# A two-layer transformer block on one core: each chunk's gelu made twice from its PSUM bank instead of once and cast

## The chip, the cores and the metric

The kernel runs on one core of one Trainium2 chip. The metric is the device time of one execution in microseconds (us), lower is better.

## The reference, cut to what matters

8192 tokens (128 sequences of 64) of width 256 pass through two layers. Each has a modulated layer norm, attention with 16 heads over the 64 tokens of a sequence, a projection with a residual, a second modulated norm and a feed-forward part of width 1024 (the second layer rotates queries and keys too):

```python
z = z * (1.0 + gamma2[:, None, :]) + beta2[:, None, :]
z = jax.nn.gelu(z @ fc1_w + fc1_b, approximate=False) @ fc2_w + fc2_b
x = x + z * alpha2[:, None, :]
```

## The kernel before

A tile is 512 tokens, so there are 16 tiles in each layer, numbered 0 to 31 through both. Each engine has one hand-written program; semaphores join them, and the order of the work on an engine is the order of the calls in its `step`. Step u does three things side by side: attention of tile u, the feed-forward part of tile u-1 (its last back product falls in step u+1), and the norm and the query, key and value products of tile u+1. Steps are unrolled at the ends of a layer and looped between. The argument named `a` is the layer of tile u+1, `b` that of tile u, `c` that of tile u-1, and None where there is no such tile.

Every matrix product is done in three passes: operands are split into a high part, rounded to fp32r, and a low part, the rest; high by high, high by low and low by high are added.

The hidden layer goes in 8 chunks of 128 channels. For chunk m:

- PE's `hidden` (L1086; its matmuls stand under L912) makes 6 matmuls of 512 columns into bank C, the only bank for it. It waits until the gelu of chunk m-1 has read C (semaphore `gelu`).
- ACT's `hidden` (L754) makes `hact` from C with the bias, at L757. `hact`, `h_hi` and `h_lo` hold two chunks each, in turn.
- ACT's `hidden_high` (L759) casts `hact` to `h_hi` at L762. It waits on the gelu's semaphore and on the back product of chunk m-2.
- POOL's `hidden_low` (L556) makes `h_lo = hact - h_hi` at L559.
- PE's `back` (L1095) makes 12 matmuls of 256 columns into banks D: 8 with `h_hi`, then, after a wait for `h_lo`, 4 with it (L1106).

In ACT's `step`, the cast stands right behind its gelu for chunks 1, 5, 6 and 7. For chunks 0, 2, 3 and 4 there is other work between. What matters around them:

- `high_heads` (L777) writes the high part of the turned heads, `ot_hi`, from bank E; DVE's `low_heads` (L1406) then writes `ot_lo`, and PE's `project` (L912, into E) waits for both.
- `exponential` (L766) of one half-group of attention scores, before PE's `turn_probs` (L1050) transposes them into B.
- `move_probs` (L771) copies the turned probabilities out of B to `probs_turned`; PE's `weigh_values` (L1064) waits for it.
- `high_qk` (L738 in the first layer) writes `q_flat` or `k_flat`; DVE's `low_qk` (L1345) follows, and holds what stands behind it on DVE.

PE runs, around chunks 0 and 1: `hidden` 0, `project` 0, two `first_turn`s, `turn_heads` 1, `hidden` 1, `project` 1, `back` 0, `hidden` 2. Around chunk 3: `hidden` 3, `turn_probs` (2,0), `queries_keys` 1, `turn_probs` (2,1), `back` 2, `weigh_values` (2,0) and (2,1).

Of the kernel before, what the change touches and what calls it, by code (L numbers as in the profile page):

```python
# [34 lines left out]
ACT = mybir.ActivationFunctionType  # L35
# [7 lines left out]
MC = FF // P  # L43
# [23 lines left out]
def build(nc, t, out):  # L67

    ctx = ExitStack()
    with ctx:  # L70
        def sb(name, shape, dt=F32):
            return ctx.enter_context(nc.sbuf_tensor(name, shape, dt))

        def bank(name):
            return ctx.enter_context(nc.psum_tensor(name, [P, 512], F32))

        def sem(name):
            return ctx.enter_context(nc.semaphore(name))
# [46 lines left out]
        hact = sb("hact", [P, 2, TILE])  # L125
        hb = [sb("h_hi", [P, 2, TILE], F32R), sb("h_lo", [P, 2, TILE], F32R)]
# [8 lines left out]
        b1_col = sb("b1_col", [P, 2, MC])  # L135
# [35 lines left out]
        C = bank("C")  # L171
# [37 lines left out]
        pe_f1, gelu, h_hi, h_lo, pe_f2 = sem("pe_f1"), sem("gelu"), sem("h_hi"), sem("h_lo"), sem("pe_f2")  # L209
# [5 lines left out]
        def upto(u, n, k):  # L215
            return u * n + k

        def known(u):
            return isinstance(u, int)

        def await_(eng, semaphore, count):

            if not (known(count) and count <= 0):
                eng.wait_ge(semaphore, count)
# [288 lines left out]
        def _(pool):  # L513
# [42 lines left out]
            def hidden_low(tile, m):  # L556
                await_(pool, pe_f2, upto(tile, MC, m - 1))
                pool.wait_ge(h_hi, upto(tile, MC, m + 1))
                pool.tensor_tensor(hb[1][:, m % 2, :], hact[:, m % 2, :], hb[0][:, m % 2, :].bitcast(F32),  # L559
                                   ALU.subtract).then_inc(h_lo, 1)  # L560

# [46 lines left out]
            def step(u, n, a, b, c, p):  # L608
                if c is not None:
                    second_rstd(u - 1, G - 1)  # L610
                if p is not None:
                    hidden_low(u - 2, MC - 2)
# [46 lines left out]
        def _(act):  # L659
# [43 lines left out]
            def second_norm(tile, g):  # L703
                await_(act, pe_zt, upto(tile - 1, 2, g // 2 + 1))
                act.wait_ge(ln2_rstd, upto(tile, G, g + 1))
                nc.scalar.activation(zn[:, g, :], x_res[:, g, :], ACT.Identity, scale=rs2[:, g:g + 1],
                                     bias=nb2[:, g:g + 1]).then_inc(zn_ready, 1)
# [44 lines left out]
                        nc.scalar.copy(dst, src).then_inc(v_moved, 1)  # L752

            def hidden(tile, layer, m):  # L754
                act.wait_ge(pe_f1, upto(tile, MC, m + 1))
                await_(act, h_lo, upto(tile, MC, m - 1))
                nc.scalar.activation(hact[:, m % 2, :], C[:, :], ACT.Gelu, bias=b1_col[:, layer, m:m + 1]).then_inc(gelu, 1)  # L757

            def hidden_high(tile, m):  # L759
                act.wait_ge(gelu, upto(tile, MC, m + 1))  # L760
                await_(act, pe_f2, upto(tile, MC, m - 1))
                nc.scalar.copy(hb[0][:, m % 2, :], hact[:, m % 2, :]).then_inc(h_hi, 1)  # L762

            def exponential(u, g, b):
                act.wait_ge(s_sub, upto(u, 2 * G, 2 * g + b + 1))
                nc.scalar.activation(exps[:, b, :], exps[:, b, :], ACT.Exp, scale=SCORE_SCALE).then_inc(s_exp, 1)  # L766
# [13 lines left out]
            def step(u, n, a, b, c, p):  # L780
                if p is not None:
                    hidden(u - 2, p, MC - 1)
                    hidden_high(u - 2, MC - 1)
                if c is not None:
                    second_norm(u - 1, G - 1)
                if b is not None:
                    exponential(u, 0, 0)
                if c is not None:
                    second_high(u - 1, 0)
                if b is not None:  # L790
                    exponential(u, 0, 1)
                    move_probs(u, 0, 0)
                    move_probs(u, 0, 1)
                if known(u) and u == NT:
                    act.wait_ge(pe_proj, upto(NT, G, 0))
                    high_weights(1, 1)
                if known(u) and u == NT + 1:
                    high_piece(2, 1, 3)
                    high_piece(3, 1, 2)
                if b is not None:  # L800
                    exponential(u, 1, 0)
                    exponential(u, 1, 1)
                    move_probs(u, 1, 0)
                if c is not None:
                    second_high(u - 1, 1)
                if b is not None:
                    move_probs(u, 1, 1)
                    high_heads(u, b, 0)
                if known(u) and u == NT + 1:
                    high_piece(3, 1, 3)  # L810
                if c is not None:
                    hidden(u - 1, c, 0)
                if b is not None:
                    high_heads(u, b, 1)
                if c is not None:
                    hidden_high(u - 1, 0)
                if c is not None:
                    hidden(u - 1, c, 1)
                    hidden_high(u - 1, 1)
                if a is not None:  # L820
                    first_high(u + 1, 0)
                if b is not None:
                    second_norm(u, 0)
                if a is not None:
                    first_high(u + 1, 1)
                if c is not None:
                    hidden(u - 1, c, 2)
                if b is not None:
                    exponential(u, 2, 0)
                    second_norm(u, 1)  # L830
                    exponential(u, 2, 1)
                if c is not None:
                    hidden_high(u - 1, 2)
                if a == 0:
                    high_qk(u + 1, 0, 0)
                if c is not None:
                    hidden(u - 1, c, 3)
                if b is not None:
                    move_probs(u, 2, 0)
                if a == 0:  # L840
                    high_qk(u + 1, 0, 1)
                if b is not None:
                    move_probs(u, 2, 1)
                if c is not None:
                    hidden_high(u - 1, 3)
                if a == 1:
                    high_qk(u + 1, 1, 0)
                if b is not None:
                    exponential(u, 3, 0)
                if a == 0:  # L850
                    high_qk(u + 1, 0, 2)
                if b is not None:
                    high_heads(u, b, 2)
                if a == 1:
                    high_qk(u + 1, 1, 1)
                if b is not None:
                    move_probs(u, 3, 0)
                    exponential(u, 3, 1)
                if a == 0:
                    high_qk(u + 1, 0, 3)  # L860
                if known(u) and u == NT:
                    high_piece(2, 1, 0)
                    high_piece(2, 1, 1)
                if c is not None:
                    hidden(u - 1, c, 4)
                if b is not None:
                    move_probs(u, 3, 1)
                if a == 1:
                    high_qk(u + 1, 1, 2)
                if c is not None:  # L870
                    hidden_high(u - 1, 4)
                if b is not None:
                    second_norm(u, 2)
                if a == 1:
                    high_qk(u + 1, 1, 3)
                if a is not None:
                    values(u + 1, 0)
                if c is not None:
                    hidden(u - 1, c, 5)
                    hidden_high(u - 1, 5)  # L880
                if b is not None:
                    high_heads(u, b, 3)
                if known(u) and u == NT:
                    high_piece(3, 1, 0)
                if a is not None:
                    values(u + 1, 1)
                if c is not None:
                    hidden(u - 1, c, 6)
                    hidden_high(u - 1, 6)
                if known(u) and u == NT - 2:  # L890
                    act.wait_ge(pe_v, upto(NT, 2, 0))
                    high_weights(0, 1)
                if known(u) and u == NT:
                    high_piece(3, 1, 1)
                    high_piece(2, 1, 2)
                if n is not None:
                    first_norm(u + 2)
                    first_columns(u + 2, n)
                if b is not None:
                    second_columns(u, b)  # L900
# [729 lines left out]
```

## Time and profile before

| | |
|---|---|
| median of 3 runs | 1885.76 us (1884.67 to 1885.84) |
| the profiled execution's own time | 1885.72 us |
| its span | 1883.9 us |
| granted clock | 0.986 |
| PE busy / DVE / ACT / POOL | 95% / 66% / 69% / 45% |

The span runs from the first to the last instruction of the profiled execution; 1.8 us of its time lie outside. Times in rows are from the span's start. PE is the matmul engine, PEld its weight loads, ACT the scalar engine, DVE the vector engine. A busy share is an average over steps, and says little by itself where an engine waits.

### The profile page before, as it was taken

What the parts mean: (1) busy time and instruction counts of PE and PEld (TensorE: products, weight loads), DVE (VectorE), ACT (ScalarE), POOL (GpSimd) and SP (SyncE); (2) the same over time, 40 slices, a digit from 0 to 9 for tenths busy, and PEclk for the clock granted to TensorE, in tenths of its full rate; (3) what the DMA queues carried; (4) which work ended last, traced back from release to release, by engine and by line L of the source; (5) the groups of instructions that cost most, each with busy time, mean ns of one, the idle gap of its engine ahead of it and who ended that gap; (6) DMA issues with size and microseconds to landing.
All of it is one profiled execution on the core that took longest, in us unless ns stands there. A gap on an engine that the chain in (4) does not pass through costs nothing.

```text
span 1883.9 us, 41740 instructions
## 1 busy us (share of the span) xinstructions
PE 1788.1 (95%) x12623; PEld 1637.1 (87%) x12623; DVE 1237.4 (66%) x2985; ACT 1306.7 (69%) x2327; POOL 849.4 (45%) x1036
## 2 busy tenths in 40 slices
PE   4779999999999999999899999999999999999998
PEld 3668888888988888988889999999999999999986
DVE  4756667667667667666867667667667766666751
ACT  4337777777776776776668776776776677777663
POOL 2123333333333343333456655555665555566534
PEclk8889999999999999999999999999999999999999
DMA  6463435454434444344454233334323333333320
GB/s 166 107 147 95 100 97 133 117 128 111 97 96 119 122 122 122 89 105 108 124 149 109 84 108 98 98 107 114 84 86 105 101 103 106 103 84 97 93 71 34
DMA packets 330276, 199.84 MB, mean 106 GB/s; under 512 B 160995, under 2 KB 314597, under 8 KB 330213
## 3 DMA queue, kind: packets, MB, share of 16 engines
q1 hardware_dynamic: 330212, 199.06, 40.0%
q8 instruction: 32, 0.52, 0.1%
q14 instruction: 32, 0.25, 0.0%
HBM read 80.98 MB, written 17.33 MB: 52 GB/s over the span
## 4 chain that ended last, share of the span: by engine, by line
PE 73%; DVE 12%; issue 8%; SPq 2%; ACT 2%; DMA 1%; POOL 1%; DVEq 0%; POOLq 0%; ACTq 0%
PE D L1106 17%; PE C L912 16%; PE B L912 9%; PE B L1064 9%; PE A L1031 7%; PE B L1050 5%; PE A L912 5%; PE E L912 4%; DVE mx L1373 2%; SPq L329 2%; DVE o_sb L1397 2%; PE A L1036 2%; DVE exps L1379 1%; DVE ot_lo L1406 1%; PE E L1075 1%
## 5 line engine op out<-in xcount | busy, mean ns | idle before, releaser
L559 POOL TENSOR_TENSOR h_lo<-hact,h_hi 128x512 fp32r<-128x512 f32 x256 | 330.4, 1291 | 302.6 <-ACT h_hi L762 289.5
L1031 PE MATMUL A<-k_pad,q_pad 128*128 128x256 f32 x1536 | 259.9, 296 | 14.3 <-DVE exps L1379 9.3
L1106 PE MATMUL D<-wgt_hi,h_hi 128*128 128x256 f32 x1024 | 263.4, 290 | 0.0
L771 ACT COPY probs_turned<-B 128x512 f32<-128x512 f32 x256 | 147.7, 584 | 157.7 <-PE B L1050 157.7
L1064 PE MATMUL B<-v_blocks,probs_turned 128*128 128x68 f32 x2048 | 255.8, 272 | 0.4 <-ACT probs_turned L771 0.4
L1106 PE MATMUL D<-wgt_lo,h_hi 128*128 128x256 f32 x1024 | 255.7, 282 | 0.0
L1064 PEld LDWEIGHTS B<-v_blocks,probs_turned 128*128 128x128 f32 x2048 | 250.3, 193 | 5.8 <-ACT probs_turned L771 2.5
L757 ACT ACTIVATE hact<-C,b_col 128x512 f32<-128x512 f32 x256 | 176.1, 688 | 96.0 <-PE C L912 92.1
L1031 PEld LDWEIGHTS A<-k_pad,q_pad 128*128 128x128 f32 x1536 | 214.8, 194 | 18.3 <-issue 9.5
L1373 DVE TENSOR_REDUCE mx<-A 128x8 f32<-128x512 f32 x256 | 174.3, 681 | 69.3 <-PE A L1036 39.4
L766 ACT ACTIVATE exps<-exps 128x512 f32<-128x512 f32 x256 | 160.9, 630 | 76.3 <-DVE exps L1379 75.7
L1106 PEld LDWEIGHTS D<-wgt_lo,h_hi 128*128 128x128 f32 x1024 | 195.4, 191 | 1.4
L1106 PEld LDWEIGHTS D<-wgt_hi,h_hi 128*128 128x128 f32 x1024 | 194.7, 190 | 2.1 <-ACT h_hi L762 0.4
L1379 DVE TENSOR_TENSOR exps<-A,mx 128x512 f32<-128x512 f32 x256 | 174.1, 680 | 4.0 <-PE B L1050 0.7
L912 PE MATMUL C<-z_hi,wgt_hi 128*128 128x512 f32 x512 | 168.9, 411 | 5.3 <-ACT hact L757 4.8
L549 POOL TENSOR_SCALAR rs<-mv 128x1 f32<-128x1 f32 x128 | 28.3, 221 | 316.0 <-DVE mv L1430 304.7
L1106 PE MATMUL D<-wgt_hi,h_lo 128*128 128x256 f32 x1024 | 166.6, 285 | 1.5 <-POOL h_lo L559 1.3
L1050 PE MATMUL B<-ident,exps 128*128 128x128 f32 x1024 | 157.5, 277 | 6.4 <-DVE q_flat L1345 1.4
L762 ACT CAST h_hi<-hact 128x512 fp32r<-128x512 f32 x256 | 159.4, 623 | 4.2
L1397 DVE TENSOR_TENSOR o_sb<-B,rden 64x128 f32<-64x128 f32 x512 | 146.5, 286 | 23.1 <-PE E L1075 5.8
L912 PE MATMUL C<-z_hi,wgt_lo 128*128 128x512 f32 x512 | 159.8, 393 | 0.0
L912 PE MATMUL C<-z_lo,wgt_hi 128*128 128x512 f32 x512 | 158.8, 391 | 0.0
(140 smaller groups left out, 3944.0 us busy)
## 6 DMA issues: line engine op xcount, KB each, us to landing
k_pad<-k_flat SPq DMA_DIRECT2D x512, 64.0 KB, 2.1
q_pad<-q_flat SPq DMA_DIRECT2D x256, 128.0 KB, 2.3
gates<-gates SPq DMA_DIRECT2D x64, 256.0 KB, 4.5
x_bias<-x_bias SPq DMA_DIRECT2D x32, 512.0 KB, 3.5
rotation<-rotation SPq DMA_DIRECT2D x256, 64.0 KB, 1.9
x_in<-in_x SPq DMA_DIRECT2D x16, 512.0 KB, 4.2
gates<-gated_bias SPq DMA_DIRECT2D x32, 256.0 KB, 5.0
x_res<-in_x SPq DMA_DIRECT2D x16, 512.0 KB, 4.4
```

Of the source, the lines that this page charges most:

```text
L559: pool.tensor_tensor(hb[1][:, m % 2, :], hact[:, m % 2, :], hb[0][:, m % 2, :].bitcast(F32), ALU.subtract).then_inc(h_lo, 1)
L757: nc.scalar.activation(hact[:, m % 2, :], C[:, :], ACT.Gelu, bias=b1_col[:, layer, m:m + 1]).then_inc(gelu, 1)
L762: nc.scalar.copy(hb[0][:, m % 2, :], hact[:, m % 2, :]).then_inc(h_hi, 1)
L766: nc.scalar.activation(exps[:, b, :], exps[:, b, :], ACT.Exp, scale=SCORE_SCALE).then_inc(s_exp, 1)
L912: ins = nc.tensor.matmul(dst, l[p], r[q], start=(p, q) == order[0] and n == 0, stop=(p, q) == order[-1] and n == len(pairs) - 1)
L1031: ins = nc.tensor.matmul(dst, qpad[g % 2][:, c, p, b, :, :].rearrange("p x s -> p (x s)"), kpad[g % 2][:, c, q, :, b * S:(b + 1) * S], sta ...
L1050: ins = nc.tensor.transpose(B[b][:, n * P:(n + 1) * P], exps[:, b, n * P:(n + 1) * P], ident[:, :])
L1064: ins = nc.tensor.matmul(B[b][:, n * 68:(n + 1) * 68], pt[:, b, n * P:(n + 1) * P], moving, start=True, stop=True)
L1106: ins = nc.tensor.matmul(Dk[g // 2][:, (g % 2) * D:(g % 2 + 1) * D], hb[p][:, m % 2, g * P:(g + 1) * P], w_slice(q, W_FF2, D, m, 0, D), st ...
L1373: nc.vector.tensor_reduce(mx[:, b, :], A[b][:, :].rearrange("p (h k) -> p h k", k=S), AX.X, ALU.max)\
L1379: nc.vector.tensor_tensor(exps[:, b, :].rearrange("p (h k) -> p h k", k=S), A[b][:, :].rearrange("p (h k) -> p h k", k=S), mx[:, b, :].rea ...
L1397: ins = nc.vector.tensor_tensor(o_sb[p, b, :].rearrange("p (n j d) -> p n j d", n=4, j=2), sums_of(b)[p, :, x, :, 0:HD], rden[p, b, :].rea ...
```

## The change

ACT's `hidden` now reads bank C twice. The first gelu writes `h_hi` directly, rounded, and signals `h_hi`; the second writes `hact`, unrounded, and signals `gelu`, which frees C. `hidden_high` with its cast is gone, and so are its eight call sites. The first gelu takes the wait for the back product of chunk m-2 that the cast had; the second keeps the wait for `h_lo` of chunk m-2. POOL's `hidden_low` waits for both gelus.

```diff
             def hidden_low(tile, m):
                 await_(pool, pe_f2, upto(tile, MC, m - 1))
                 pool.wait_ge(h_hi, upto(tile, MC, m + 1))
+                pool.wait_ge(gelu, upto(tile, MC, m + 1))
...
             def hidden(tile, layer, m):
+
                 act.wait_ge(pe_f1, upto(tile, MC, m + 1))
+                await_(act, pe_f2, upto(tile, MC, m - 1))
+                nc.scalar.activation(hb[0][:, m % 2, :], C[:, :], ACT.Gelu, bias=b1_col[:, layer, m:m + 1]).then_inc(h_hi, 1)
                 await_(act, h_lo, upto(tile, MC, m - 1))
                 nc.scalar.activation(hact[:, m % 2, :], C[:, :], ACT.Gelu, bias=b1_col[:, layer, m:m + 1]).then_inc(gelu, 1)
-
-            def hidden_high(tile, m):
-                act.wait_ge(gelu, upto(tile, MC, m + 1))
-                await_(act, pe_f2, upto(tile, MC, m - 1))
-                nc.scalar.copy(hb[0][:, m % 2, :], hact[:, m % 2, :]).then_inc(h_hi, 1)
...
                 if b is not None:
                     high_heads(u, b, 1)
                 if c is not None:
-                    hidden_high(u - 1, 0)
-                if c is not None:
                     hidden(u - 1, c, 1)
-                    hidden_high(u - 1, 1)
...
                 if b is not None:
                     move_probs(u, 2, 1)
-                if c is not None:
-                    hidden_high(u - 1, 3)
```

The other call sites go the same way. The first place is on ACT in the loop of the first layer, around chunk 0: the gelu out of C, the heads' high part (`ot_hi`) and the cast, and then chunk 1's gelu. Before:

```order
L757 ACT_TABLE_LOAD
L757 ACTIVATE hact<-C,b_col 128x512 [waits h_lo]
L774 REGISTER_ALU
L777 ACTIVATE ot_hi<-E,v_bias 128x128 [waits pe_proj,pe_ot]
L777 ACTIVATE ot_hi<-E,v_bias 128x128
L762 CAST h_hi<-hact 128x512 [waits pe_f2,gelu]
L755 REGISTER_ALU
L757 ACTIVATE hact<-C,b_col 128x512 [waits h_lo,pe_f1]
```

And now:

```order
L759 ACT_TABLE_LOAD
L759 ACTIVATE h_hi<-C,b_col 128x512 [waits pe_f2]
L761 ACTIVATE hact<-C,b_col 128x512 [waits h_lo]
L773 REGISTER_ALU
L776 ACTIVATE ot_hi<-E,v_bias 128x128 [waits pe_proj,pe_ot]
L776 ACTIVATE ot_hi<-E,v_bias 128x128
L757 REGISTER_ALU
L759 ACTIVATE h_hi<-C,b_col 128x512 [waits pe_f2,pe_f1]
```

The second reading of C has moved in front of the heads, and the cast behind them is gone.

The second place is ACT in the same loop around chunk 3: the gelu, the two copies of turned probabilities with a key chunk (`k_flat`) between them, the cast, and the next exponential. Before:

```order
L757 ACT_TABLE_LOAD [waits h_lo]
L757 ACTIVATE hact<-C,b_col 128x512 [waits pe_f1]
L771 COPY probs_turned<-B 128x512 [waits pe_pv,pe_pt]
L736 REGISTER_ALU
L738 ACTIVATE k_flat<-A,qk_bias 128x4x128 [waits pe_qk]
L771 COPY probs_turned<-B 128x512 [waits pe_pv,pe_pt]
L762 CAST h_hi<-hact 128x512 [waits pe_f2,gelu]
L765 REGISTER_ALU
L766 ACT_TABLE_LOAD
L766 ACTIVATE exps<-exps 128x512 [waits s_sub]
```

And now:

```order
L759 ACT_TABLE_LOAD [waits pe_f2]
L759 ACTIVATE h_hi<-C,b_col 128x512 [waits pe_f1]
L761 ACTIVATE hact<-C,b_col 128x512 [waits h_lo]
L770 COPY probs_turned<-B 128x512 [waits pe_pv,pe_pt]
L737 REGISTER_ALU
L739 ACTIVATE k_flat<-A,qk_bias 128x4x128 [waits pe_qk]
L770 COPY probs_turned<-B 128x512 [waits pe_pv,pe_pt]
L764 REGISTER_ALU
L765 ACT_TABLE_LOAD
L765 ACTIVATE exps<-exps 128x512 [waits s_sub]
```

A gelu has come in ahead of both copies and the key chunk, and the cast behind them is gone. The number of table loads in the program is the same, 54.

## Rows read from the trace of the kernel before

**Rows 1.** The page: busy time, and the chain that ended last

```profile
PE 1788.1 (95%) x12623; PEld 1637.1 (87%) x12623; DVE 1237.4 (66%) x2985; ACT 1306.7 (69%) x2327; POOL 849.4 (45%) x1036
PE 73%; DVE 12%; issue 8%; SPq 2%; ACT 2%; DMA 1%; POOL 1%; DVEq 0%; POOLq 0%; ACTq 0%
```

**Rows 2.** Groups by line on ACT (busy us, mean ns, idle before)

```profile
L757 ACT ACTIVATE hact<-C,b_col 128x512 f32<-128x512 f32 x256 | 176.1, 688 | 96.0 <-PE C L912 92.1 <-POOL h_lo L559 1.5
L762 ACT CAST h_hi<-hact 128x512 fp32r<-128x512 f32 x256 | 159.4, 623 | 4.2
```

**Rows 3.** Waits of PE after 960 us (total, times, longest)

```profile
PE C L912 <- ACT hact L757: 4.8, 15, 0.8
...
PE D L1106 <- POOL h_lo L559: 0.7, 3, 0.2
```

**Rows 4.** Timeline of ACT, second layer, chunk 0 (start, us long)

```profile
1314.84 0.69 ACT L757 ACTIVATE hact<-C,b_col 128x512 f32<-128x512 f32 x1
1315.43 0.62 ACT L777 ACTIVATE ot_hi<-E,v_bias 128x128 fp32r<-128x128 f32 x2
```

**Rows 5.** Timeline of PE, second layer, `hidden` 1 in two steps

```profile
1093.73 0.74 PE L912 MATMUL C<-z_hi,wgt_hi 128*128 128x512 f32 x2 [0.24 <-ACT hact L757]
...
1315.59 0.73 PE L912 MATMUL C<-z_hi,wgt_hi 128*128 128x512 f32 x2 [0.24 <-ACT hact L757]
```

**Rows 6.** Timeline, first layer, chunk 0: ACT, then PE's `hidden` 1

```profile
411.66 0.69 ACT L757 ACTIVATE hact<-C,b_col 128x512 f32<-128x512 f32 x1
...
413.46 0.71 PE L912 MATMUL C<-z_hi,wgt_hi 128*128 128x512 f32 x2
```

**Rows 7.** Timeline of ACT, first layer, from chunk 2's cast on

```profile
422.82 0.60 ACT L762 CAST h_hi<-hact 128x512 fp32r<-128x512 f32 x1
...
425.32 0.69 ACT L757 ACTIVATE hact<-C,b_col 128x512 f32<-128x512 f32 x1
425.91 0.58 ACT L771 COPY probs_turned<-B 128x512 f32<-128x512 f32 x1
...
426.95 0.59 ACT L771 COPY probs_turned<-B 128x512 f32<-128x512 f32 x1
```

**Rows 8.** Timeline of PE in the same stretch

```profile
426.95 1.90 PE L1064 MATMUL B<-v_blocks,probs_turned 128*128 128x68 f32 x16
...
427.80 1.05 PE L1064 MATMUL B<-v_blocks,probs_turned 128*128 128x68 f32 x8
...
433.45 0.65 PE L1050 MATMUL B<-ident,exps 128*128 128x128 f32 x4
```

**Rows 9.** Timeline of DVE in the same stretch

```profile
427.11 0.75 DVE L1345 SCALAR_TENSOR_TENSOR k_flat<-A,qk_bias,k_flat 128x512 fp32r<-128x512 f32 x1 [2.31 <-ACT k_flat L738]
428.00 0.21 DVE L1389 RECIPROCAL rden<-B 128x8 f32<-128x8 f32 x1
...
432.57 0.75 DVE L1345 SCALAR_TENSOR_TENSOR q_flat<-B,qk_bias,q_flat 128x512 fp32r<-128x512 f32 x1 [1.28 <-ACT q_flat L738]
```

**Rows 10.** Timeline, first layer, step's start, PE

```profile
454.86 0.63 PE L1050 MATMUL B<-ident,exps 128*128 128x128 f32 x4
...
467.08 0.48 PE L912 MATMUL E<-wgt_hi,ot_hi 128*128 128x256 f32 x2 [0.89 <-DVE ot_lo L1406]
```

**Rows 11.** Timeline of the last 65 us: PE, then ACT

```profile
1823.41 0.63 PE L1050 MATMUL B<-ident,exps 128*128 128x128 f32 x4 [0.38 <-ACT exps L766]
...
1855.18 0.73 PE L912 MATMUL C<-z_hi,wgt_hi 128*128 128x512 f32 x2 [0.78 <-ACT hact L757]
...
1858.10 0.63 PE L912 MATMUL C<-z_hi,wgt_hi 128*128 128x512 f32 x2
...
1854.44 0.69 ACT L757 ACTIVATE hact<-C,b_col 128x512 f32<-128x512 f32 x1 [1.75 <-PE C L912]
1855.16 0.62 ACT L762 CAST h_hi<-hact 128x512 fp32r<-128x512 f32 x1
1856.88 0.69 ACT L757 ACTIVATE hact<-C,b_col 128x512 f32<-128x512 f32 x1 [1.09 <-PE C L912]
```

More of the change, by code:

```diff
@@ L782, in step @@
                     hidden(u - 2, p, MC - 1)
-                    hidden_high(u - 2, MC - 1)
                 if c is not None:
@@ L831, in step @@
                     exponential(u, 2, 1)
-                if c is not None:
-                    hidden_high(u - 1, 2)
                 if a == 0:
@@ L843, in step @@
                     move_probs(u, 2, 1)
-                if c is not None:
-                    hidden_high(u - 1, 3)
                 if a == 1:
@@ L869, in step @@
                     high_qk(u + 1, 1, 2)
-                if c is not None:
-                    hidden_high(u - 1, 4)
                 if b is not None:
@@ L879, in step @@
                     hidden(u - 1, c, 5)
-                    hidden_high(u - 1, 5)
                 if b is not None:
@@ L888, in step @@
                     hidden(u - 1, c, 6)
-                    hidden_high(u - 1, 6)
                 if known(u) and u == NT - 2:
```

## Prediction, made before the changed kernel ran

> **What bounds the kernel now.** I read the busy shares and the chain first. PE is busy for 95% of the span, and the chain that ended last lies on PE for 73% and on DVE for 12%; ACT has 2% of it [rows 1]. So the time is PE's, and an edit on ACT counts only where PE waits for it, or where it comes to. Next the waits of PE. In the first layer none is for a gelu. After 960 us there are 15 waits for the gelu that frees bank C, 4.8 us in all [rows 3]. The timeline shows where. In the second layer PE's `hidden` 1 starts at 1315.59, 0.24 us idle, and the gelu of chunk 0 ends at 1314.84 + 0.69 = 1315.53 [rows 4, 5]. The same row with the same idle stands in each of twelve steps, from 1093.73 on [rows 5]; the other three are in the last 65 us, one of them at 1855.18 [rows 11]. So in those steps the wait on bank C already ends last, with nothing in reserve. In the first layer the gelu of chunk 0 ends at 411.66 + 0.69 = 412.35 and PE uses C again at 413.46, 1.11 us later [rows 6].
>
> **What the change removes and adds on ACT.** It takes away 256 casts of 623 ns and adds 256 gelus out of the bank of 688 ns [rows 2]. The trace has no gelu behind a gelu. An instruction behind one starts 0.59 us after it if it waits for nothing (425.32 to 425.91 [rows 7], 1314.84 to 1315.43 [rows 4]); where it waits for the gelu's semaphore, as the cast does, it starts 0.72 us after (1854.44 to 1855.16 [rows 11]). The second gelu waits for no result of the first, so I take 0.59, and 0.72 is the upper bound. A cast cost ACT its 0.60 [rows 7] less the 0.10 by which an unhindered successor begins before the end (425.32 + 0.69 - 425.91), so 0.50. Per chunk that is +0.09 where other work stood between, and 0.13 less, -0.04, where the cast stood right behind. ACT's load is thus the same; what changes is where the time lies.
>
> The Trainium skill's page "ScalarE: Activation LUTs" (section "What ACT_TABLE_LOAD costs") gives an ACTIVATE with a pointer bias 280 ns + 0.833 ns per column, and an overlap of 93 ns between two in a row. That is 706 - 93 = 613 ns for the added gelu, an estimate from the page; the row says 590 and stands. By the page the sum below would be 0.6 us larger.
>
> Who gets what: the high part comes sooner everywhere, and the low part about as soon as before in chunks 1, 5, 6, 7 and sooner in the others. PE hardly waits for either, so this earns next to nothing. The price is that bank C, and everything behind the gelu on ACT, is released 0.59 us later. The wait for the back product of chunk m-2, now ahead of the first gelu, costs nothing: PE issues that product before `hidden` m, whose end the gelu waits for anyway.
>
> **Second layer, chunk 0.** PE's `hidden` 1 starts when the second gelu ends: 1314.84 + 0.59 + 0.69 = 1316.12, and 0.06 for the start, 1316.18 instead of 1315.59: +0.59. Behind the gelu on ACT stand the heads' high parts, due at 1315.43; 0.59 later they are still ready for `project` 1, which PE reaches after `hidden` 1, itself 0.59 later. PE runs almost without a gap after that, and what DVE, POOL and the DMAs do for it next starts from PE's own products, so they shift with it. Twelve steps: 12 x 0.59 = **7.1 us** (upper bound 12 x 0.72 = 8.6).
>
> **First layer, chunk 0.** 1.11 us of cover against 0.59: nothing.
>
> **First layer, chunk 3.** Here the gelu holds up the copies of turned probabilities. ACT arrives at the gelu of chunk 3 later by 0.59 (second gelu of chunk 2) less 0.50 (its cast, gone from 422.82 [rows 7]) = 0.09. Then a second gelu: the copies and the key chunk between them all come 0.59 + 0.09 = 0.68 later. The first copy ends at 425.91 + 0.58 = 426.49 and PE's `weigh_values` starts at 426.95; the second ends at 426.95 + 0.59 = 427.54 and its matmuls start at 427.80 [rows 7, 8]. Cover of 0.46 and 0.26 is less than 0.68: PE's second block starts at 427.54 + 0.68 + 0.05 = 428.27, +0.47. DVE says the same: its `low_qk` waits for the key chunk (2.31 us idle), goes from 427.11 to 427.79 and ends at 428.54, and the reciprocal behind it, at 428.00 [rows 9], starts at about 428.5, +0.5. I take 0.47. From there the chain runs over the normalised heads, the next maximum and subtraction, the exponential and the query chunk to DVE's `low_qk` at 432.57 [rows 9], for which PE waits before it turns probabilities at 433.45 [rows 8]. So the 0.47 reaches PE again and isn't taken back. After this PE runs gapless to the start of the next step, and DVE's long chain there starts from PE's first scores. Steps 1 to 14 have this order (the loop and its two unrolled ends): 14 x 0.47 = **6.6 us**. Lower bound 0, if that cover is larger than I read; upper 14 x 0.68 = 9.5.
>
> In the second layer ACT has no key chunk between the copies, since `high_qk` stands later, and they come early enough: nothing.
>
> **First layer, step's start.** ACT has no idle time before the first exponential, and two gelu-cast pairs stand in that stretch, so it comes about 0.1 us sooner, and PE waits for it at 454.86. But PE waits 0.89 us for DVE at 467.08 [rows 10]; DVE works without a gap from the first scores on. What PE gains at 454.86 it waits longer at 467.08: nothing.
>
> **The end, after 1822 us.** PE waits for the exponential at 1823.41 [rows 11], which comes 0.59 later, and for the copy behind it, 0.68 later in all: +0.7. Three waits for the gelu, of 15 [rows 3], grow by 0.59 each: +1.8. In the last tile nothing but the feed-forward part is left. There the gelu of chunk 1 ends at 1856.88 + 0.69 = 1857.57 and PE needs C at 1858.10 [rows 11]: cover of 0.53 against 0.59 + 0.05. So chunks 1, 2, 5 and 6 wait about 0.1 each: +0.4. The last two low parts come 0.05 sooner: -0.1. Together **+2.8 us**, bounds 2 and 4.5.
>
> **Sum.** 7.1 + 6.6 + 2.8 = 16.5 us. The profiled execution took 1885.72 us (span 1883.9, 1.8 outside), which is the median 1885.76 within its own scatter. 1885.7 + 16.5 = 1902.2; I say **1902 us**, 0.9% slower.
>
> The page "PSUM — Partial Sum Buffer" of the Trainium skill (summary of rules) says to evacuate promptly. It speaks against this change, and the trace agrees: bank C is the one that PE waits for at 1315.59.
>
> **Rivals.**
> *A: the first layer's stall is covered.* For it: the cover of 0.46 and 0.26 is no small part of 0.68, and DVE was 2.31 us idle before that chunk. Against it: DVE's own queue arrives at the same +0.47. Time: 1885.7 + 7.1 + 2.8 = 1895.6. Chance 0.10.
> *B: the second gelu doesn't overlap the first.* 0.72 instead of 0.59 in 12 + 14 steps and some 6 places of the end: 32 x 0.13 = 4.2 more, 1906. For it: only different instructions are seen behind a gelu. Chance 0.10.
> *C: not slower, by the sooner `h_hi` and `h_lo`.* PE has some waits for `h_lo`, 0.7 us in all in the second layer [rows 3], and the first layer's first exponential comes sooner. It decides only if bank C isn't held longer, so if both readings together end no later than the one gelu, which 2 x 0.69 less an overlap of 0.10 rules out unless the second reading is shortened. Time: 0.7 + 14 x 0.1 = 2.1 less, 1884, or a little below. Chance 0.03.
> *D: no difference.* PE is later at chunk 0, but catches up in the same step at waits that are set by something which doesn't shift. Against it: the rows show PE without such waits in the second layer. Time 1886. Chance 0.03.
> My forecast has the rest, 0.74, and its own range is 1898 to 1905.
>
> **How the numbers follow.** 0.2% of 1886 us, 3.8 us, is about what a measurement of this kernel can tell from no change. Range: from A, 1895.6 with its end at the lower bound, 1895, to B, 1906, plus a little for the end: 1895 to 1907. It leaves out C and D and the tails, under 2 in 10. Slower 0.94; same 0.04 (D, and a part of C); faster 0.02 (the rest of C).
>
> **What the new profile would show.** Right: the second gelu starts 0.59 after the first; in twelve steps of the second layer PE idles about 0.8 us before `hidden` 1, for `hact`; in steps 1 to 14 PE waits for `probs_turned` at `weigh_values` (2,1); steps of the first layer are 0.47 us longer, and those of the second 0.59 (four of them now take 1315.59 - 1093.73 = 221.9 us [rows 5], which becomes 224.2). Wrong, if the step length of either layer is unchanged, or if POOL or DVE became what PE waits for.

## The result, and the profile after

The changed kernel takes 1900.09 us (median of 4 runs, 1898.91 to 1900.92). The kernel before, run on the same chip, takes 1885.22 us (median of 4, 1884.59 to 1885.84). The ratio is 1.0077, with a 95% interval of 1.0063 to 1.0090: 14.9 us slower. Forecast were 1902 us and slower. The profiled execution of the changed kernel has a span of 1897.5 us, 13.6 us more than before; the granted clock of TensorE has the same mean of 0.986 in both, so the clock explains nothing of it.

The changed kernel's page first: busy times, then the chain that ended last, then the two groups of `hidden` on ACT (busy us, mean ns of one, idle time before and what ended it).

```profile
PE 1792.6 (94%) x12623; PEld 1639.3 (86%) x12623; DVE 1235.9 (65%) x2985; ACT 1307.9 (69%) x2327; POOL 850.1 (45%) x1036
...
PE 67%; DVE 12%; issue 10%; ACT 7%; SPq 3%; DMA 1%; POOL 1%; DVEq 0%; ACTq 0%; POOLq 0%
...
L759 ACT ACTIVATE h_hi<-C,b_col 128x512 fp32r<-128x512 f32 x256 | 176.3, 689 | 137.4 <-PE C L899 134.0
L761 ACT ACTIVATE hact<-C,b_col 128x512 f32<-128x512 f32 x256 | 174.4, 681 | 0.0
```

ACT has the same number of instructions as before and is busy for 1.2 us more in 1307.9: its load is not what costs. Its share of the chain that ended last went from 2% to 7% [rows 1]. The second group has no idle time before it, so the second reading of the bank always stands right behind the first. The next rows are the first lines of PE's waits after 960 us in the changed kernel (total us, times, longest).

```profile
PE C L899 <- ACT hact L761: 13.3, 15, 1.4
...
PE B L1051 <- ACT probs_turned L770: 1.0, 1, 1.0
```

The same 15 waits for the gelu as before, 8.5 us more in all [rows 3]. The timeline at the first of the two places, second layer, chunk 0: ACT, then PE.

```profile
1320.00 1.28 ACT L759 ACT_TABLE_LOAD   x1 [1.71 <-PE C L899]
1321.30 0.69 ACT L759 ACTIVATE h_hi<-C,b_col 128x512 fp32r<-128x512 f32 x1
1321.88 0.68 ACT L761 ACTIVATE hact<-C,b_col 128x512 f32<-128x512 f32 x1
1322.45 0.63 ACT L776 ACTIVATE ot_hi<-E,v_bias 128x128 fp32r<-128x128 f32 x2
```

```profile
1322.61 0.73 PE L899 MATMUL C<-z_hi,wgt_hi 128*128 128x512 f32 x2 [0.81 <-ACT hact L761]
1323.18 0.63 PE L899 MATMUL C<-z_hi,wgt_lo 128*128 128x512 f32 x2
1323.65 0.62 PE L899 MATMUL C<-z_lo,wgt_hi 128*128 128x512 f32 x2
1324.11 0.40 PE L899 MATMUL E<-wgt_hi,ot_hi 128*128 128x256 f32 x2
1324.35 0.40 PE L899 MATMUL E<-wgt_lo,ot_hi 128*128 128x256 f32 x2
```

The second gelu starts 0.58 us after the first and ends at 1322.56; PE's `hidden` 1 starts 0.05 later, 0.81 us idle instead of 0.24 [rows 5].

The second place, first layer, chunk 3, on ACT, PE and DVE:

```profile
426.64 0.69 ACT L759 ACTIVATE h_hi<-C,b_col 128x512 fp32r<-128x512 f32 x1
427.23 0.68 ACT L761 ACTIVATE hact<-C,b_col 128x512 f32<-128x512 f32 x1
427.80 0.58 ACT L770 COPY probs_turned<-B 128x512 f32<-128x512 f32 x1
428.26 0.71 ACT L739 ACTIVATE k_flat<-A,qk_bias 128x512 fp32r<-128x512 f32 x1
428.85 0.60 ACT L770 COPY probs_turned<-B 128x512 f32<-128x512 f32 x1
```

```profile
426.68 0.36 PE L1093 MATMUL D<-wgt_hi,h_hi 128*128 128x256 f32 x1
...
428.53 2.08 PE L1051 MATMUL B<-v_blocks,probs_turned 128*128 128x68 f32 x16 [0.17 <-ACT probs_turned L770]
...
435.16 0.65 PE L1037 MATMUL B<-ident,exps 128*128 128x128 f32 x4
```

```profile
429.01 0.75 DVE L1332 SCALAR_TENSOR_TENSOR k_flat<-A,qk_bias,k_flat 128x512 fp32r<-128x512 f32 x1 [2.90 <-ACT k_flat L739]
429.68 0.20 DVE L1376 RECIPROCAL rden<-B 128x8 f32<-128x8 f32 x1
```

`weigh_values` (2,0) now waits 0.17 us for the first copy, and the 16 matmuls of (2,0) and (2,1) take 2.08 instead of 1.90 us [rows 8]. The ninth matmul, the first of (2,1), starts at 429.50, 0.05 after the end of the second copy. About 0.11 of the 0.18 lies there and 0.07 at the first matmul: a short wait in the middle of a group shows as a longer group. DVE was idle for 2.90 us before the key chunk instead of 2.31 [rows 9].

How long is a step? The start of the gelu of chunk 0 in `hact` marks it. Two such rows, ten steps apart, first for the first layer and then for the second (ACT):

```profile
244.38 0.68 ACT L761 ACTIVATE hact<-C,b_col 128x512 f32<-128x512 f32 x1
...
808.05 0.68 ACT L761 ACTIVATE hact<-C,b_col 128x512 f32<-128x512 f32 x1
...
1154.01 0.68 ACT L761 ACTIVATE hact<-C,b_col 128x512 f32<-128x512 f32 x1
...
1713.83 0.68 ACT L761 ACTIVATE hact<-C,b_col 128x512 f32<-128x512 f32 x1
```

(808.05 - 244.38) / 10 = 56.37 us, and (1713.83 - 1154.01) / 10 = 55.98. The same rows of the kernel before stand at 243.85, 803.18, 1148.48 and 1703.15, which makes 55.93 and 55.47. So a step of the first layer is 0.44 us longer and one of the second 0.51. Added up over the trace, with each tile's first gelu as the mark (in the changed kernel the one into `h_hi`, 0.58 us ahead of the other; the steps have the same length by either): the steps into tiles 1 to 13 +5.7, those into tiles 14 to 17 (the change of layer) -0.3, the twelve of the second layer +6.1, from the first gelu of tile 29 to the end of the program +3.0, and the time before tile 0's first gelu -0.9. That is the span's 13.6. The -0.9 at the start isn't the change's, since no changed instruction runs before that gelu; over the kernels below, chunk 0's gelu of tile 1 stands anywhere between 185.3 and 189.3 us. The change of layer scatters too: e12 below runs the same instructions there as the changed kernel, and its steps into tiles 14 to 17 are 1.2 us longer than before where the changed kernel's are 0.3 shorter. Without the start the terms make 14.5, beside 14.9 by the medians.

In the last 65 us these waits of PE have grown:

```profile
1837.59 0.63 PE L1051 MATMUL B<-v_blocks,probs_turned 128*128 128x68 f32 x4 [1.00 <-ACT probs_turned L770]
...
1848.76 0.73 PE L899 MATMUL C<-z_hi,wgt_hi 128*128 128x512 f32 x2 [0.92 <-ACT hact L761]
...
1867.52 0.73 PE L899 MATMUL C<-z_hi,wgt_hi 128*128 128x512 f32 x2 [1.36 <-ACT hact L761]
...
1881.49 0.73 PE L899 MATMUL C<-z_hi,wgt_hi 128*128 128x512 f32 x2 [1.36 <-ACT hact L761]
```

The wait of 0.78 at 1855.18 [rows 11] is the one that now stands at 1867.52 with 1.36 us: +0.58, one second gelu. The kernel before has the other two at 1836.99 (0.34) and 1868.21 (0.78), and each grew by 0.58 as well.

### The profile page after: what moved, and what is told of

Same layout as the page of the kernel before. It is cut to its first block, busy times and chain, and to the rows that moved or that the text cites. A ratio compares the mean times of both kernels' runs of the same rounds, so it can differ in the third digit from the quotient of the medians.

```text
span 1897.5 us, 41684 instructions
## 1 busy us (share of the span) xinstructions
PE 1792.6 (94%) x12623; PEld 1639.3 (86%) x12623; DVE 1235.9 (65%) x2985; ACT 1307.9 (69%) x2327; POOL 850.1 (45%) x1036
## 4 chain that ended last, share of the span: by engine, by line
PE 67%; DVE 12%; issue 10%; ACT 7%; SPq 3%; DMA 1%; POOL 1%; DVEq 0%; ACTq 0%; POOLq 0%
PE C L899 15%; PE D L1093 14%; PE B L899 9%; PE B L1051 9%; PE A L1018 7%; PE E L899 4%; PE B L1037 4%; PE A L899 3%; SPq L329 2%; DVE mx L1360 2%; ACT hact L761 2%; DVE o_sb L1384 2%; PE A L1023 1%; DVE exps L1366 1%; DVE ot_lo L1393 1%
## 5 line engine op out<-in xcount | busy, mean ns | idle before, releaser
L759 ACT ACTIVATE h_hi<-C,b_col 128x512 fp32r<-128x512 f32 x256 | 176.3, 689 | 137.4 <-PE C L899 134.0
```

What stands on the lines that cost most here:

```text
L759: nc.scalar.activation(hb[0][:, m % 2, :], C[:, :], ACT.Gelu, bias=b1_col[:, layer, m:m + 1]).then_inc(h_hi, 1)
```

## The experiments

All were timed in five rounds beside the kernel before, and compared by ratio. Step lengths are read as above, ten steps apart, from each kernel's own trace. The theory is that of the prediction: three places, and at each of them a delay by one gelu. Here are all twelve together; "longer" is the ratio less 1, times 1885.5 us, the middle of the medians of the kernel before.

| kernel | median us | ratio, 95% interval | longer, us | step, first layer | step, second layer |
|---|---|---|---|---|---|
| before | 1885.2 to 1886.0 | | | 55.93 | 55.47 |
| changed | 1900.09 | 1.0077 [1.0063, 1.0090] | +14.5 | 56.37 | 55.98 |
| e1 chunk 0 by cast | 1893.63 | 1.0045 [1.0031, 1.0058] | +8.5 | 56.36 | 55.47 |
| e2 chunk 3 by cast | 1893.35 | 1.0042 [1.0028, 1.0056] | +7.9 | 55.91 | 56.00 |
| e3 chunks 0, 3 by cast | 1885.83 | 1.0003 [0.9994, 1.0012] | +0.6 | 55.91 | 55.47 |
| e4 second gelu 3 late | 1893.46 | 1.0040 [1.0026, 1.0053] | +7.5 | 55.91 | 55.99 |
| e5 bank held only | 1892.81 | 1.0037 [1.0025, 1.0050] | +7.0 | 55.91 | 55.97 |
| e6 delay only | 1889.76 | 1.0026 [1.0016, 1.0036] | +4.9 | 56.34 | 55.46 |
| e7 changed, table early | 1894.00 | 1.0050 [1.0037, 1.0063] | +9.4 | 56.33 | 55.48 |
| e8 e4, table early | 1887.09 | 1.0008 [0.9999, 1.0017] | +1.5 | 55.87 | 55.44 |
| e9 before, table early | 1885.35 | 1.0000 [0.9991, 1.0009] | 0 | 55.89 | 55.49 |
| e10 e9, low heads first | 1877.74 | 0.9961 [0.9947, 0.9975] | -7.4 | 55.58 | 55.19 |
| e11 e8, low heads first | 1877.92 | 0.9960 [0.9946, 0.9974] | -7.5 | 55.59 | 55.20 |
| e12 end by cast | 1898.15 | 1.0062 [1.0048, 1.0076] | +11.7 | 56.37 | 55.99 |

**e1, e2 and e3: undo one part of the change.** In the chunks of `CAST` the high part is the cast of before again, at its old place; the others read the bank twice. e1 has `CAST = (0,)`, e2 `(3,)`, e3 `(0, 3)`.

```diff
+                if m not in CAST:
+                    await_(act, pe_f2, upto(tile, MC, m - 1))
+                    nc.scalar.activation(hb[0][:, m % 2, :], C[:, :], ACT.Gelu, ...).then_inc(h_hi, 1)
...
+            def hidden_high(tile, m):
+                if m in CAST:
+                    act.wait_ge(gelu, upto(tile, MC, m + 1))
+                    await_(act, pe_f2, upto(tile, MC, m - 1))
+                    nc.scalar.copy(hb[0][:, m % 2, :], hact[:, m % 2, :]).then_inc(h_hi, 1)
```

> The changed kernel, with chunk 0 alone made in the old way (one gelu out of bank C, and the cast at its old place); the other seven chunks read the bank twice. My theory: the second layer's loss is the bank held 0.58 us longer at chunk 0, in 12 steps, so PE's wait before hidden 1 falls from 0.81 to 0.24 us there, and one of the waits in the last tile too: 1900.1 - 12 x 0.51 - 0.6 = 1893.4 us. The first layer's steps stay 56.37 us long. Rival, that any chunk's second reading costs its share alike (14.9 us over eight chunks): 1900.1 - 1.9 = 1898.2.

> The changed kernel, with chunk 3 alone made in the old way. My theory: the first layer's loss is the 0.68 us by which the copies of turned probabilities and the key chunk behind the gelu of chunk 3 come later, so its steps fall from 56.37 to 55.93 us in 14 steps, and the second layer's stay at 56.0: 1900.1 - 14 x 0.44 = 1893.9, some 0.5 less with what it gives at the end, 1893.5 us. Rival, an equal share for each chunk: 1898.2. Rival A of the prediction (that stall is covered, and the 6 us came from elsewhere in the first layer): 1900.

> The changed kernel, with chunks 0 and 3 made in the old way. My theory: both losses of the steady steps go, 12 x 0.51 + 14 x 0.44 + 1.1 at the end = 13.4 of the 14.9 us: 1886.7 us, with steps of 55.93 and 55.47 us as before, and what is left lies after 1822 us. Rival, an equal share for each chunk: 1900.1 - 3.7 = 1896.4.

Measured: 1893.63, 1893.35 and 1885.83 us. The step lengths separate cleanly. With chunk 0 by cast the second layer's step is that of before (55.47) and the first layer's stays long; with chunk 3 by cast it is the other way round; with both, six of eight chunks read the bank twice and the time is 0.6 us longer by the ratio, with an interval of -1.1 to +2.3 that holds no difference. So in the steady steps the double reading costs nothing where it has cover, and the two losses are separate and add up. What is left lies at the end: from tile 29's first gelu on, e3 takes 1.9 us longer than before.

**e4: all chunks twice, but chunk 3's second gelu late.** It stands where the cast stood, behind the two copies and the key chunk.

```diff
+                if m not in LATE:
+                    gelu_low(tile, layer, m)
...
+            def hidden_high(tile, layer, m):
+                if m in LATE:
+                    gelu_low(tile, layer, m)
```

> Every chunk reads the bank twice, but chunk 3's second gelu stands where its cast stood, behind both copies and the key chunk. Bank C isn't wanted again for 10.9 us there. If the loss of the first layer is the place in ACT's queue, its steps fall to 55.93 us: 1900.1 - 14 x 0.44 - 0.5 = 1893.5 us, as with the cast. Rival, that it is the second reading of the bank itself, or ACT's 65 ns more per chunk: no change, 1900.

Measured: 1893.46 us. The first layer's step is back at 55.91, although bank C is read twice in every chunk and, at chunk 3, held longer than in the changed kernel. ACT in that stretch:

```profile
424.84 0.69 ACT L765 ACTIVATE h_hi<-C,b_col 128x512 fp32r<-128x512 f32 x1
425.42 0.58 ACT L784 COPY probs_turned<-B 128x512 f32<-128x512 f32 x1
425.89 0.70 ACT L739 ACTIVATE k_flat<-A,qk_bias 128x512 fp32r<-128x512 f32 x1
426.47 0.59 ACT L784 COPY probs_turned<-B 128x512 f32<-128x512 f32 x1
426.94 0.72 ACT L759 ACTIVATE hact<-C,b_col 128x512 f32<-128x512 f32 x1
```

The first copy starts 0.58 us after the gelu again (0.59 before), instead of 1.16. At chunk 3 it is the queue on ACT that costs, not the bank.

**e5: hold the bank, and nothing else.** The kernel before; in the second layer PE's `hidden` 1 also waits for the heads' high part, which ACT makes right behind the gelu.

```diff
-            def hidden(tile, m):
+            def hidden(tile, m, held=False):
...
+                if m == 1 and held:
+                    pe.wait_ge(ot_hi, upto(tile + 1, 8, 4))
...
-                    hidden(u - 1, 1)
+                    hidden(u - 1, 1, held=c == 1 and b is not None)
```

> The kernel before with one wait more: in the second layer PE's hidden 1 (the first write of bank C after chunk 0's gelu) also waits for ot_hi of heads 1, which ACT ends about 0.51 us after that gelu. ACT's instructions and their order are those of before, so only the bank is held longer. Theory of the prediction (in the second layer the loss is the bank held at chunk 0): 12 steps of about 0.5 us, 1885.6 + 6.1 = about 1891.5 us. Rival (the loss is ACT's queue moved later, ot_hi and what follows it, and not the bank): 1885.6 us, no difference.

Measured: 1892.81 us; the interval of the ratio, +4.7 to +9.4 us, holds the theory's 6.1 and not the rival's 0. The second layer's step is 0.50 longer. The edit holds the bank in 15 steps and not in the theory's 12: three steps (tiles 16, 29 and 30) in which neither kernel waits for the bank at chunk 0 wait here too and are some 0.5 us longer. That fits the measured 7.0 beside 6.1. In PE's timeline (the waits after 960 us below it) the imitated wait looks like the changed kernel's 0.81:

```profile
1318.97 0.70 PE L912 MATMUL C<-z_hi,wgt_hi 128*128 128x512 f32 x2 [0.84 <-ACT ot_hi L777]
```

```profile
PE C L912 <- ACT ot_hi L777: 12.5, 15, 0.8
```

At chunk 0 the held bank is enough to make the whole loss of a step: ACT has its work of before in the order of before.

**e6: delay, and nothing else.** The kernel before, with one more gelu on ACT in the first layer, from SBUF into a tile that nobody reads, between chunk 3's gelu and the copies.

```diff
+                if c is not None and a == 0:
+                    nc.scalar.activation(spare[:, :], mod[:, 0, 0, :, :, :].rearrange("p k s b -> p (k s b)"), ACT.Gelu, bias=b1_col[:, c, 3:4])
```

> The kernel before with one 512-column gelu more, from a tile in SBUF into a spare tile, between chunk 3's gelu and the copies of probs_turned in the 14 steps of the first layer that have the stall. The bank is read once and released as before, POOL's low part comes from the same tile as before; only what stands behind on ACT is 0.58 to 0.59 us later than without it. Theory of the prediction (the first layer loses by the later copies and key chunk, until the cover is used up): 14 steps of 0.38 to 0.44 us, 1885.6 + 5.3 to 6.2 = 1890.9 to 1891.8 us. Rival A (the low heads' stall covers it): 1885.6 us.

Measured: 1889.76 us. The interval, +3.0 to +6.8 us, excludes rival A's 0 and holds the theory's 5.3 to 6.2, though its middle of 4.9 is a little below them. The step is 0.41 longer, inside the 0.38 to 0.44. On ACT:

```profile
428.31 0.69 ACT L758 ACTIVATE hact<-C,b_col 128x512 f32<-128x512 f32 x1
428.89 0.71 ACT L840 ACTIVATE spare<-mod,b_col 128x512 f32<-128x512 f32 x1
429.50 0.57 ACT L772 COPY probs_turned<-B 128x512 f32<-128x512 f32 x1
```

The bank is read once here. With e4 this makes the case for chunk 3 from both sides: the delay alone costs nearly what the change costs (0.41 of 0.44 us a step), and the double reading without the delay costs nothing. In e6 chunk 3's cast comes later as well, which in the changed kernel nothing does; but PE's waits for `h_hi` and `h_lo` over the whole program stay small, 1.7 us instead of 1.3.

**e7 and e9: bring the table load forward.** ACT loads its gelu table (1.28 us) at the gelu of chunk 0. In the changed kernel's rows above it starts after 1.71 us of idle time, when PE has ended `hidden` 0. A gelu of one column ahead of it takes the load into ACT's idle time. e7 is the changed kernel with it, e9 the kernel before.

```diff
+        warm = sb("warm", [P, 1])
...
+                if c is not None and b is not None:
+                    nc.scalar.activation(warm[:, :], b1_col[:, c, 0:1], ACT.Gelu)
```

> The changed kernel with a 1-column gelu into a spare tile ahead of each tile's hidden 0, so that ACT loads its table (1.28 us) while PE still works on hidden 0 and not after it. Both gelus of chunk 0 then end about 1.2 us earlier, and bank C is free before PE comes to it, though read twice. Theory of the prediction (second layer: bank C at chunk 0 costs about 0.5 us a step): the 12 steps come back to the length that they have before the change, where DVE's low heads take the wait over: 1900.1 - 6.1 = about 1894 us. Rival (the time is lost to ACT's work itself, not to the bank's release): 1900 us or more, since ACT has one instruction more a tile.

> The kernel before with the 1-column gelu ahead of hidden 0 alone. Bank C is free 1.2 us earlier at chunk 0, but project 1's matmul then waits for DVE's low part of the attention's output, which comes some 0.1 us before PE restarts today. Theory: no difference or a gain under 0.1 us a step, 1884.5 to 1885.6 us. Rival (the bank alone sets the restart): 12 x 0.24 = 2.9 us less, 1882.7 us.

Measured: 1894.00 and 1885.35 us. ACT in e7:

```profile
1317.12 1.28 ACT L811 ACT_TABLE_LOAD   x1
1318.41 0.20 ACT L811 ACTIVATE warm<-b_col 128x1 f32<-128x1 f32 x1
1318.84 0.69 ACT L760 ACTIVATE h_hi<-C,b_col 128x512 fp32r<-128x512 f32 x1 [0.22 <-PE C L902]
1319.43 0.68 ACT L762 ACTIVATE hact<-C,b_col 128x512 f32<-128x512 f32 x1
```

And PE's `hidden` 1 in e7, with no idle time before it:

```profile
1320.38 0.71 PE L902 MATMUL C<-z_hi,wgt_hi 128*128 128x512 f32 x2
```

The second gelu ends at 1320.11, 0.27 before PE wants the bank. The second layer's step is 55.48, that of before. In e9 the same cure earns nothing, though the wait of 0.24 for the bank [rows 5] is gone; PE in e9:

```profile
1314.88 0.71 PE L915 MATMUL C<-z_hi,wgt_hi 128*128 128x512 f32 x2
...
1316.83 0.47 PE L915 MATMUL E<-wgt_hi,ot_hi 128*128 128x256 f32 x2 [0.31 <-DVE ot_lo L1409]
```

The wait has moved to `project` 1, which needs DVE's low part of the heads. So the 0.24 us at the bank could be taken away, and PE gained nothing by it.

**e8: both cures.** e4 with the one-column gelu; its edits are those shown above.

> All chunks twice from the bank, with both cures: chunk 3's second gelu stands where the cast stood before (behind the copies and the key chunk), and a 1-column gelu ahead of hidden 0 brings the table load forward. Theory: both losses are gone, 1893.46 - 6.1 = about 1887.5 us, that is the kernel before but for the end of the program (about 2 us). Rival (reading the bank twice costs by itself): 1893 us or more.

Measured: 1887.09 us, with an interval of -0.2 to +3.2. Both step lengths are those of before or a little less, though ACT makes every chunk's gelu twice. From tile 29's first gelu to the end it still takes 2.4 us longer than before.

**e10 and e11: the wait behind the waits.** On DVE the low part of heads 1 goes ahead of the next tile's `y_scale` and of the second aggregate. e10 is e9 with it, e11 is e8 with it.

```diff
+                if b is not None:
+                    low_heads(u, b, 1)
                 if a is not None:
                     y_scale(u + 1, 0)
                 if b is not None:
                     second_aggregate(u, 0)
-                    low_heads(u, b, 1)
```

> The kernel before with the 1-column gelu ahead of hidden 0, and on DVE the low part of heads 1 ahead of the next tile's y_scale and the second aggregate. If project 1's wait for ot_lo is what PE loses in the first layer (about 0.5 us a step, 14 steps) and, with the table load out of the way, in the second (0.2 to 0.39 us, 12 steps), it gives 1885.6 - 5 to 9.6 = 1876 to 1881 us. Rival (the moved work of DVE is late for PE at once after it, and the wait only goes there): 1885 us or more.

> All chunks twice from the bank with both cures and the same order of DVE as the run of the kernel before that puts the low heads first. Theory: the double reading then costs only the end of the program, about 2 us more than that run: 1878 to 1883 us. Rival (double reading eats what DVE's order gives): 1885 us or more.

Measured: 1877.74 and 1877.92 us, 7.4 and 7.5 less than before: the fastest kernels here. PE and DVE in e10:

```profile
1310.23 0.71 PE L915 MATMUL C<-z_hi,wgt_hi 128*128 128x512 f32 x2
...
1311.93 0.47 PE L915 MATMUL E<-wgt_hi,ot_hi 128*128 128x256 f32 x2
```

```profile
1311.17 0.61 DVE L1409 SCALAR_TENSOR_TENSOR ot_lo<-E,v_bias,ot_hi 128x128 fp32r<-128x128 f32 x2 [0.31 <-ACT ot_hi L778]
```

From `hidden` 1 to `project` 1 it is 1.70 us instead of e9's 1.95, and the step is 0.29 shorter. DVE now waits 0.31 us for ACT's high part, and PE no longer waits at this `project` 1.

More than half of e10's gain lies in the first layer, where the bank isn't waited for at all. In the kernel before, PE waits 0.36 us for the low part of heads 1 at `project` 1 of each step there:

```profile
415.46 0.36 PE L912 MATMUL E<-wgt_hi,ot_hi 128*128 128x256 f32 x1 [0.36 <-DVE ot_lo L1406]
```

e9 has the same wait (0.36), e10 doesn't have it, and the first layer's step is 0.31 us shorter than e9's. DVE's order alone, without the table load brought forward, wasn't run, so how much of the 7.4 us it gives by itself is not shown.

e11 was expected about 2 us above e10, at 1878 to 1883, and came out 0.2 above it and just under that range. Each interval reaches 2.6 us either way, so the times can't tell 0.2 from 2. The steps of the two are the same within 0.01 us, and from tile 29's first gelu to the end e11 takes 2.5 us longer: the steady steps don't pay for the double reading here, the end still does.

**e12: undo the change at the end.** The changed kernel, with the cast back in tiles 30 and 31 only.

```diff
+            CAST_FROM = 30
...
+                if not (known(tile) and tile >= CAST_FROM):
...
+                if known(tile) and tile >= CAST_FROM:
```

> The changed kernel, but in the last two tiles of the program (30 and 31, both of the second layer) the high part is the cast of before again, at its old place. Theory of the prediction (at the end each chunk of the last tiles waits for both gelus, +2.8 us forecast, about 2.5 us between chunk 0 of tile 29 and the end in the two traces): 1900.1 - 2.5 = about 1897.6 us. Rival (the end lies behind another wait and gives nothing): 1900.1 us.

Measured: 1898.15 us, 1.9 less than the changed kernel's median and 2.8 less by the ratios; the two intervals overlap, so the times alone don't settle a term of this size. The trace does. From tile 29's first gelu to the end of the program it takes what the kernel before takes, within 0.01 us, and 3.0 less than the changed kernel. (The 2.5 of the expectation counts from the gelu into `hact`, which in the changed kernel comes 0.58 later.) In PE's waits after 960 us the three long ones have shrunk:

```profile
PE C L919 <- ACT hact L763: 11.6, 15, 0.8
```

## Why the prediction was right

**The whole.** The median is 1900.09 where 1902 was said, and the loss 14.9 where the sum was 16.5. The place, the sign and the mechanism of each large term held; two of the three sizes were a little large.

**Second layer, chunk 0: said 12 x 0.59 = 7.1 us, measured 12 x 0.51 = 6.1.** e1, e5 and e7 show the cause: undoing chunk 0 removes this term alone, holding the bank alone makes it, giving the bank cover removes it. The term was sized too large by 0.08 a step. The rows account for it: PE starts 0.57 later, not 0.59 (idle 0.81 instead of 0.24), and something is won back at `project` 1. In the kernel before its first pair of matmuls took 0.29 us to the next pair; in the changed kernel it is 1324.35 - 1324.11 = 0.24, where DVE's low part has been there for 0.39 us and not for 0.17. The rows of before:

```profile
1317.08 0.45 PE L912 MATMUL E<-wgt_hi,ot_hi 128*128 128x256 f32 x2
1317.37 0.40 PE L912 MATMUL E<-wgt_lo,ot_hi 128*128 128x256 f32 x2
```

That the 0.05 comes from this is read from the two traces and wasn't tried by itself.

**First layer, chunk 3: said 14 x 0.47 = 6.6 us, measured 5.7 in the 13 steps into tiles 1 to 13, 0.44 each.** e2 removes it alone, e4 removes it with all gelus still doubled, e6 makes it by delay alone. PE turns the next probabilities at 435.16, 8.48 after the first back product of that stretch at 426.68. In the kernel before that product starts at 425.43, and the probabilities are turned at 433.45 [rows 8], 8.02 later: +0.46.

```profile
425.43 0.36 PE L1106 MATMUL D<-wgt_hi,h_hi 128*128 128x256 f32 x1
```

Whether the fourteenth step loses as well can't be read. The step into tile 14 grew by 0.27 in the changed kernel, by 0.0 in e1 and by 1.15 in e12, which all have the same chunk 3 there. One sign was placed wrongly: PE's recorded wait for `probs_turned` comes at (2,0), for the first copy, and the forecast had it at (2,1). There the second copy holds PE too, but only inside the group.

**First layer, chunk 0, and the step's start: said nothing.** With chunk 3 put right (e2) the first layer's step is 55.91 against 55.93, so both cost nothing.

**The end: said 2.8, measured 3.0**, and e12 gives it back. Inside this sum two small terms were sized wrongly. Chunks 1, 2, 5 and 6 of the last tile cost 0.6 us together and not 0.4: PE's next `hidden` starts 3.00 to 3.03 us after the one before it instead of 2.81 to 2.94. And the low parts, forecast to give 0.1 back, gave nothing back.

**The spacing of two gelus** was taken from other pairs of instructions as 0.59; the trace has 0.58 to 0.59. The estimate of 613 ns from the Trainium skill's page "ScalarE: Activation LUTs" (section "What ACT_TABLE_LOAD costs") was 27 ns too high: the second gelu takes 681 ns and starts 586 ns after the first. The same page's overlap of 93 ns between two ACTIVATEs in a row agrees with the rows: 0.69 - 0.59 = 0.10.

**The rivals.** A (the first layer's stall is covered): refuted by e6 and by the step of 56.37. B (no overlap of the two gelus, 1906): refuted by the spacing of 0.58 to 0.59. C and D (no loss): refuted by the times. The rule to evacuate promptly on the page "PSUM — Partial Sum Buffer" of the Trainium skill (summary of rules) gives the small size of PSUM as its reason, and no price. Here a longer hold of one bank cost time at chunk 0 of the second layer and in the last 65 us, where PE waits for that bank. Elsewhere it didn't: where PE comes back to the bank over 1 us later [rows 6], 0.59 us of holding costs nothing (the first layer of e4), and at chunk 3 the loss comes from ACT's queue, since e4 holds the bank for longer still and loses nothing there.

## What to carry to other kernels

An exchange that leaves an engine's load alone can still cost: read for each place which resource is released later, who wants it next, and by how much it comes early, and multiply only where the cover is smaller than the delay. A wait that looks like a free gain may have another just behind it. Here, in the second layer, the bank's 0.24 us hid DVE's 0.31: the table load brought forward gave nothing by itself (e9), and with the low heads first as well the kernel was 7.4 us faster (e10). The low heads first without the table load wasn't tried. Losses read in this way add up from place to place, so they can be undone one at a time; one gelu moved and a one-column gelu added (e8) took back all but 1.5 us of the double gelu's cost (-0.2 to +3.2) without undoing it.

## What the runs showed of the hardware

- ACT's table load waited here with the gelu that needed it. In the changed kernel the load of 1.28 us at chunk 0 starts when PE's matmul into C ends, after 1.71 us of idle time on ACT. A one-column gelu of 0.20 us in front takes it off the path of the bank.
- A gelu of 512 columns takes 689 ns in front and 681 ns directly behind another; 586 ns pass between their starts. With 623 ns for the cast from SBUF [rows 2], the double reading costs ACT almost the same time as gelu and cast.
- A short wait inside a group of matmuls can be missing from the wait column: the two `weigh_values` grew from 1.90 to 2.08 us, about 0.11 of it at the ninth matmul, which starts 0.05 us after the second copy ends, with no wait recorded there.
